# A five-part rewrite of the first stage of a graph network kernel: where the small factor's products, the zeros and the angles are computed

## The reference, cut to what matters

```python
h = jnp.maximum(_layernorm(x, axis=-1), 0.0)
x = x + L0(h)      # h @ W_conv (512x128), summed over edges with dinv*w*dinv, + b_conv, @ W_lin + b_lin
# for layer 2, depends on the noise levels alone:
ph = noise_levels * freqs                       # 625 x 32
emb = concatenate([sin(ph), cos(ph)])           # 625 x 64
cond = silu(emb @ f_w1 + f_b1) @ f_w2 + f_b2    # 625 x 16
```

## Time and profile before

| what | value |
|---|---|
| three runs | 974.55, 974.86, 977.94 us, median 974.86 |
| profiled execution, its own time | 974.24 us |
| its span | 972.2 us |
| mean granted TensorE clock | 0.967 of full |
| busy share of the span | PE 88%, DVE 69%, POOL 53%, ACT 46% |
| chain that ended last | PE 56%, DVE 20%, POOL 7%, issue 6%, ACT 5% |

### The profile page before, as it was taken

One profiled execution on the slowest core, in us unless ns is written; L12 is line 12 of the kernel. 1 busy time (PEld: TensorE's weight loads), 2 busy tenths in 40 slices (PEclk: granted clock), 3 DMA queues, 4 the chain that ended last, 5 costly groups with the idle time before them and its releaser, 6 DMA issues.

```text
span 972.2 us, 18314 instructions
## 1 busy us (share of the span) xinstructions
PE 860.0 (88%) x6780; PEld 752.3 (77%) x6780; DVE 672.2 (69%) x1311; ACT 451.4 (46%) x760; POOL 519.3 (53%) x598
## 2 busy tenths in 40 slices
PE   0799976998999989999989999989999998889787
PEld 0498875886989877999877898878798988765456
DVE  8689978786267676356577337677526767779986
ACT  1277754323466233456323347522346625245564
POOL 6357744345843176753266663236684319537771
PEclk9999997999999999999999999999999999978998
DMA  4000000204310016220003430001431002100111
GB/s 114 23 23 0 0 22 22 68 16 104 98 34 1 1 34 162 68 65 1 1 22 101 113 104 2 1 22 52 125 102 31 1 1 76 33 1 28 42 56 53
DMA packets 49362, 44.34 MB, mean 46 GB/s; under 512 B 6014, under 2 KB 37154, under 8 KB 49300
## 3 DMA queue, kind: packets, MB, share of 16 engines
q1 hardware_dynamic: 47124, 40.20, 14.2%
q10 hardware_dynamic: 2176, 3.32, 1.8%
HBM read 42.04 MB, written 1.33 MB: 45 GB/s over the span
## 4 chain that ended last, share of the span: by engine, by line
PE 56%; DVE 20%; POOL 7%; issue 6%; ACT 5%; DVEq 2%; SPq 2%; DMA 1%; ACTq 0%; POOLq 0%
PE psum L1583 22%; PE psum L1577 16%; PE psum L1673 8%; PE psum L1601 5%; POOL ringw L1301 3%; DVE arena L2024 2%; ACT arena L1436 2%; DVE arena L902 2%; POOL z L1216 1%; PE psum L824 1%; DVE stats L2168 1%; PE psum L1621 1%; DVEq L2269 1%; DVE hot_dst L939 1%; SPq L1142 1%
## 5 line engine op out<-in xcount | busy, mean ns | idle before, releaser
L1236 POOL TENSOR_SCALAR acc<-acc,rden,flag 128x640 f32<-128x640 f32 x80 | 70.2, 879 | 110.8 <-DVE rden L2020 110.3
L1673 PE MATMUL psum<-ringw,arena 128*128 128x512 f32 x480 | 118.9, 396 | 3.6 <-DVE arena L2032 2.5
L1583 PE MATMUL psum<-ringw,arena 128*128 128x512 f32 (+2 forms) x438 | 105.5, 399 | 12.6 <-POOL ringw L1301 5.2
L1583 PE MATMUL psum<-arena 128*128 128x384 f32 (+3 forms) x675 | 116.0, 325 | 0.4 <-DVE arena L2343 0.4
L1577 PE MATMUL psum<-arena,ringw 128*128 128x320 f32 x768 | 113.3, 309 | 0.0
L1577 PEld LDWEIGHTS psum<-arena,ringw 128*128 128x128 f32 x768 | 113.0, 188 | 0.3
L1583 PEld LDWEIGHTS psum<-arena 128*128 128x128 f32 x675 | 104.7, 189 | 7.7 <-DVE arena L2024 1.1
L1673 PEld LDWEIGHTS psum<-ringw,arena 128*128 128x128 f32 x480 | 87.8, 188 | 23.8 <-DVE arena L2032 3.5
L1583 PEld LDWEIGHTS psum<-ringw,arena 128*128 128x128 f32 x438 | 81.9, 217 | 30.3 <-issue 14.8
L1601 PE MATMUL psum<-ident,acc 128*128 128x128 f32 x560 | 82.1, 278 | 18.8 <-DVE acc L1933 14.7
L1577 PE MATMUL psum<-arena 128*128 128x320 f32 x480 | 88.5, 322 | 6.2 <-DVE arena L2024 5.5
(11 more groups left out here) (280 smaller groups left out, 1836.9 us busy)
## 6 DMA issues: line engine op xcount, KB each, us to landing
...
```

The costliest lines, as they stand in the source:

```text
L1236: g.tensor_scalar(pbuf[:, k % 4, :], pbuf[:, k % 4, :], rden[:, k:k + 1], flag[:, 1, k % NT:k % NT + 1], ALU.mult, ALU.mult).then_inc(pn_u ...
L1583: ins = pe.matmul(to, l, r, start=(i == 0), stop=(i == len(terms) - 1))
L1673: ins = pe.matmul(brow(ROWBLK[f"{name}{t}"]), l, r, start=(pieces[0] + i == 0), stop=(pieces[-1] == KT - 1 and i == len(terms) - 1))
```

## The change

- Zeros of the accumulators: from PoolE (memset) to ScalarE (copy of a broadcast column, scale 0), before its first weight.
- Noise levels load first on ScalarE's queue, without a wait; the 10 other small loads go to SyncE's queue, behind the biases and ahead of the L1 weights.
- Angles: from VectorE to PoolE, 9 instructions, ahead of `rstd_of`. ScalarE takes the absolute value of the cosine half and folds sign and shift into the sine's scale and bias.
- The fills of `fcol` become four small VectorE instructions on the identity, ahead of the edge lists.
- Norm by tile: VectorE takes statistics, normalises and splits tile by tile; TensorE turns tile t + 2 between the products of tile t (`own_features`), which now are 8 per tile, 256 columns wide (both weight parts side by side, all four terms). They lie in banks 4, 5, 6, and VectorE sums the two halves after the loop with 3 reductions (`hsum`, in SBUF), from which h0 is made; ScalarE no longer waits for VectorE there.
- z1's bias and sigmoid on ScalarE straight from PSUM, the gate product on PoolE, cond's high part on ScalarE and `condT` in one VectorE step in place of four.

```diff
-PRE_BIG = ["src", "w", "base", "dst"] + [f"l0_{t}" for t in range(NT)] + ["z1", "cond", "hall"]
+PRE_BIG = ["src", "w", "base", "dst"] + [f"l0_{t}" for t in range(NT)] + ["cond", "pad", "hall"]
...
+wave = sb("wave", [2 * NF, 2], F32)
+pick = sb("pick", [P, 6], F32)
...
+hsum = hot_dst[:, :, :, :].rearrange("p b j n -> p (b j n)").bitcast(F32)[:, NP:2 * NP].rearrange("p (t n) -> p t n", t=NT)
+cond_high = arena1[:, 0:NP]
...
+first_buf = {BIG0["l0_1"]: 0, BIG0["l0_2"]: 1, BIG0["l0_3"]: 0, BIG0["l0_4"]: 1, BIG0["cond"]: 0}
...
+def buf(u):
+    return first_buf.get(u, u % NBIG)
...
-def own_part(u, t):
...
-    return big[u % NBIG][:, t % 2, t // 2 * P:(t // 2 + 1) * P]
...
+def hall_part(t):
...
+    return psum[:, (4, 5, 4, 5, 6)[t], t // 2 % 2 * 2 * P:(t // 2 % 2 + 1) * 2 * P].rearrange("p (s n) -> p s n", s=2)
...
+z1 = psum[0:C16, 2 * NBIG:2 * NBIG + NROW, 0:HALF]
...
+    sp.wait_ge(const1, 4)
+    sp.wait_ge(cb_one, 2)
+    sp.dma_start(f_w1[:, :], a["L2_gnn_f_w1"]).then_inc(f_ld, 16)
+    sp.dma_start(fcol[0:C16, 3:4], a["L2_gnn_f_b1"].unsqueeze(1)).then_inc(f_ld, 16)
+    for i in range(4):
+        sp.dma_start(f_w2[:, 32 * i:32 * i + C16], a["L2_gnn_f_w2"]).then_inc(f_ld, 16)
+        sp.dma_start(fcol[32 * i:32 * i + C16, 2:3], a["L2_gnn_f_b2"].unsqueeze(1)).then_inc(f_ld, 16)
...
-    g.memset(acc[:, 0:NT * ACCW], 0.0).then_inc(scat_read, HOT)
-    g.memset(acc[:, NT * ACCW:2 * NT * ACCW], 0.0).then_inc(scat_full, HOT)
...
-    g.wait_ge(f_ld, 16 * F_LOADS)
-    for i in range(8):
-        if i:
-            g.wait_ge(cb_one, i)
-        g.affine_select(out=fcol[:, 2:3], in_=fcol[:, 2:3], compare_op=ALU.not_equal, fill=1.0,
-                        base=-(32 * (i // 2) + C16 + i % 2), pattern=[[0, 1]], channel_multiplier=1).then_inc(cb_one, 1)
+    for lo, sign, shift in ((0, 1.0, 0.0), (NF, -1.0, float(np.pi / 2))):
+        step(g.memset(wave[lo:lo + NF, 0:1], sign))
+        step(g.memset(wave[lo:lo + NF, 1:2], shift))
...
+    noise, ph, kf, r, part = tmp64
+    step(g.tensor_scalar(fcol[0:2 * NF, 1:2], freq_i, float(np.float32(2.0 * np.pi / 16)), 1.0, ALU.mult, ALU.mult))
+    g.wait_ge(noise_ld, 16)
+    step(g.tensor_scalar(ph, noise, fcol[0:2 * NF, 1:2], 1.0, ALU.mult, ALU.mult))
+    MAGIC = 1.5 * 2.0 ** 23
+    step(g.tensor_scalar(kf, ph, float(1 / (2 * np.pi)), MAGIC, ALU.mult, ALU.add))
+    step(g.tensor_scalar(kf, kf, -MAGIC, 1.0, ALU.add, ALU.mult))
+    TURN_HI = 6.28125
+    step(g.tensor_scalar(part, kf, -TURN_HI, 1.0, ALU.mult, ALU.mult))
+    step(g.tensor_tensor(r, part, ph, ALU.add))
+    step(g.tensor_scalar(part, kf, -float(2 * np.pi - TURN_HI), 1.0, ALU.mult, ALU.mult))
+    step(g.tensor_tensor(r, r, part, ALU.add))
+    g.tensor_scalar(r, r, 3.1415925, -3.1415925, ALU.min, ALU.max).then_inc(emb_up, 1)
...
-    for m in range(2):
-        rest(m, ringpart(m))
+        if t in (1, 2):
+            rest(t - 1, ringpart(t - 1))
+    g.wait_ge(sig_done, 1)
+    g.tensor_tensor(mask[0:C16, 3, :], mask[0:C16, 1, :], mask[0:C16, 2, :], ALU.mult).then_inc(silu_up, 1)
...
+    act.dma_start(tmp64[0][:, 0:N], a["node_vec1"].rearrange("n o -> o n").broadcast_to([2 * NF, N])).then_inc(noise_ld, 16)
+    act.wait_ge(const0, 2)
+    for i, ready in enumerate((scat_read, scat_full)):
+        act.activation(acc[:, i * NT * ACCW:(i + 1) * NT * ACCW], ones[:, 0:1].broadcast_to([P, NT * ACCW]), ACT.Copy,
+                       scale=0.0).then_inc(ready, HOT)
...
-    act.activation(tmp64[4], tmp64[3], ACT.Sin).then_inc(sin_done, 1)
+    act.activation(tmp64[3][NF:2 * NF], tmp64[3][NF:2 * NF], ACT.Abs).then_inc(sin_done, 1)
+    act.wait_ge(sin_done, 1)
+    act.activation(tmp64[4], tmp64[3], ACT.Sin, bias=wave[:, 1:2], scale=wave[:, 0:1]).then_inc(sin_done, 1)
...
+        if t == 1:
+            act.wait_ge(z1_full, 1)
+            act.wait_ge(f_ld, 16 * F_LOADS)
+            act.activation(wide(mask[0:C16, 1, :]), z1, ACT.Identity, bias=fcol[0:C16, 3:4])
+        if t == 2:
+            act.activation(wide(mask[0:C16, 2, :]), z1, ACT.Sigmoid, bias=fcol[0:C16, 3:4]).then_inc(sig_done, 1)
+    u = BIG0["cond"]
+    act.wait_ge(cb_one, 3)
+    act.wait_ge(big_full, u + 1)
+    act.activation(wide(cond_high), bwide(u), ACT.Identity, bias=pick[:, 5:6], scale=pick[:, 4:5]).then_inc(cond_hi, 1)
...
-    act.wait_ge(condT_up, 2)
...
-        if t >= 2:
-            act.wait_ge(h0lo_up, t - 1)
-        act.activation(h0[:, 0, t, :], own_part(BIG0["hall"], t), ACT.Copy, scale=degs[:, 3, t:t + 1]).then_inc(h0hi_up, 1)
+        act.activation(h0[:, 0, t, :], hsum[:, t, :], ACT.Copy, scale=degs[:, 3, t:t + 1]).then_inc(h0hi_up, 1)
...
+    u = ROW0["vec"]
+    pe.wait_ge(vec_ld, 16 * 9)
+    pe.transpose(brow(u)[:, 0:VECS], vec[:, :], ident[0:VECS, 0:VECS]).then_inc(row_full, 1)
...
-    for t in range(NT):
-        turn_norm(BIG0[f"l0_{t}"], t, t)
-    u = ROW0["vec"]
-    pe.wait_ge(vec_ld, 16 * 9)
-    pe.transpose(brow(u)[:, 0:VECS], vec[:, :], ident[0:VECS, 0:VECS]).then_inc(row_full, 1)
...
-    u = BIG0["z1"]
-    free_big(pe, u)
-    pe.wait_ge(sin_done, 1)
+    def turn_first(t):
+        pe.wait_ge(big_read, BIG0[("w", "dst", "l0_0", "l0_1", "l0_2")[t]] + 1)
+        pe.wait_ge(xn_up, t + 1)
+        turn(pe, BIG0[f"l0_{t}"], xn[:, t % 2, :], KT).then_inc(big_full, 1)
...
+    def own_features(t):
+        pe.wait_ge(big_read, BIG0[f"l0_{t}"] + 1)
+        if t == 0:
+            pe.wait_ge(split_done, Q_CONV + 1)
+        weight = ringw[:, Q_CONV, :, :].rearrange("p s (k n) -> p s k n", k=KT)
+        return row_mm(pe, hall_part(t), [(yT[:, s, k, t * P:(t + 1) * P], weight[:, :, k, :]) for k in range(KT) for s in range(2)])
...
+    turn_first(0)
+    turn_first(1)
+    pe.wait_ge(row_read, ROW0["vec"] + 1)
+    pe.wait_ge(sin_done, 2)
...
+        ins = pe.matmul(z1[:, h, :], f_w1[:, :], tmp64[4][:, h * HALF:(h + 1) * HALF], start=True, stop=True)
+    ins.then_inc(z1_full, 1)
+    own_features(0)
+    turn_first(2)
+    own_features(1)
+    turn_first(3)
+    own_features(2)
+    pe.wait_ge(sig_done, 1)
...
-    row_mm(pe, brow(u)[:, :], parts([bc_hl[:, 0, :], bc_hl[:, 1, :]], ringpart(Q_LIN))).then_inc(row_full, 1)
+    row_mm(pe, brow(ROW0["brow"])[:, :], parts([bc_hl[:, 0, :], bc_hl[:, 1, :]], ringpart(Q_LIN))).then_inc(row_full, 1)
+    turn_first(4)
+    own_features(3)
...
-    free_big(pe, u)
+    pe.wait_ge(big_read, BIG0["l0_3"] + 1)
...
-    wide_mm(pe, u, [(f_w2[:, :], mask[0:C16, 3, :])]).then_inc(big_full, 1)
...
-    u = BIG0["hall"]
-    free_big(pe, u)
-    pe.wait_ge(split_done, Q_CONV + 1)
-    pe.wait_ge(big_read, BIG0[f"l0_{NT - 1}"] + 1)
-    for t in range(NT):
-        ins = row_mm(pe, own_part(u, t), sum([parts(tile_of(yT, k, t), wcol(Q_CONV, k)) for k in range(KT)], []))
-    ins.then_inc(big_full, 1)
+    wide_mm(pe, u, [(f_w2[:, :], mask[0:C16, 3, :])]).then_inc(big_full, 2)
+    own_features(4).then_inc(big_full, 1)
...
+    dve.wait_ge(const0, 3)
+    dve.wait_ge(const1, 1)
+    blocks = ident[:, :].rearrange("p (i n) -> p i n", i=4)
+    dve.tensor_reduce(pick[:, 0:4], blocks[:, :, C16:C16 + 2], AX.X, ALU.add).then_inc(cb_one, 1)
+    dve.wait_ge(cb_one, 1)
+    dve.tensor_reduce(fcol[:, 2:3], pick[:, 0:4], AX.X, ALU.add).then_inc(cb_one, 1)
+    dve.wait_ge(cb_one, 2)
+    step(dve.tensor_reduce(pick[:, 0:4], blocks, AX.X, ALU.add))
+    step(dve.tensor_tensor(pick[:, 4:5], pick[:, 1:2], pick[:, 3:4], ALU.add))
...
+    def first_norm(t):
+        if t >= 2:
+            dve.wait_ge(big_full, BIG0[f"l0_{t - 2}"] + 1)
+        normalise(t, t, x[:, t, :], xn[:, t % 2, :])
...
+    def first_stats(t):
+        tile_stats(t, t, x[:, t, :])
...
+    def first_rest(t):
+        turned_rest(BIG0[f"l0_{t}"], t, t)
...
-    for t in range(NT):
-        tile_stats(t, t, x[:, t, :])
...
-    dve.wait_ge(const1, 3)
-    dve.wait_ge(f_ld, 16 * F_LOADS)
-    step(dve.tensor_scalar(fcol[0:2 * NF, 1:2], freq_i, float(np.float32(2.0 * np.pi / 16)), None, ALU.mult))
-    noise, ph, kf, r = tmp64[0:4]
-    step(dve.tensor_scalar(ph, noise, fcol[0:2 * NF, 1:2], None, ALU.mult))
-    MAGIC = 1.5 * 2.0 ** 23
-    step(dve.tensor_scalar(kf, ph, float(1 / (2 * np.pi)), MAGIC, ALU.mult, ALU.add))
-    step(dve.tensor_scalar(kf, kf, MAGIC, None, ALU.subtract))
-    TURN_HI = 6.28125
-    step(dve.scalar_tensor_tensor(r, kf, -TURN_HI, ph, ALU.mult, ALU.add))
-    step(dve.scalar_tensor_tensor(r, kf, -float(2 * np.pi - TURN_HI), r, ALU.mult, ALU.add))
-    step(dve.tensor_scalar(r, r, 3.1415925, -3.1415925, ALU.min, ALU.max))
-    c = r[NF:2 * NF]
-    step(dve.scalar_tensor_tensor(c, c, -1.0, c, ALU.mult, ALU.max))
-    dve.tensor_scalar(c, c, -1.0, float(np.pi / 2), ALU.mult, ALU.add).then_inc(emb_up, 1)
-    relu_norm(0, 0, [BIG0[f"l0_{t}"] for t in range(NT)], 0)
+    first_stats(0)
+    first_stats(1)
+    first_norm(0)
...
+    first_stats(2)
+    first_norm(1)
...
+    first_stats(3)
+    first_rest(0)
+    first_norm(2)
+    first_stats(4)
+    first_rest(1)
+    first_norm(3)
```

(41 more changed lines are left out.)

61 lines of the change are left out of this document (16 added, 45 removed).

## The result

The kernel after takes **962.27 us** (median of four runs, 962.08 to 962.62), the kernel before 975.48 in the same comparison (four runs, 974.55 to 977.94): ratio 0.9861, 95% interval 0.9842 to 0.988, a gain of 13.2 us. The forecast was 966.6 within 960.5 to 971.0, on the likeliest case a gain of 7.65; the gain is about that of the first rival (TensorE's clock rises inside the stage, 963.2 us) and one microsecond more: the result lies in the range, and what the forecast called likeliest did not come. The profiled execution took 962.15 us, its span is 960.3.

A forecast was written before the change was run, and what follows sets the result against it. The chain of waits to VectorE's first one-hot, then VectorE in the loop, was taken as the bound. Entry -8.5, stall -1.25 and h0 parts +2.1 gave -7.65 us on 974.24: 966.6 us, range 960.5 to 971.0.

The forecast's parts named there:

- the first rival: Stage before the loop: TensorE at 2.4 GHz from about 30 us, 3.4 us less, total 963.2 us; chance 0.25.
- Zeros and edge lists, angles: Kernel's start: zeros free 4.4 us, used up covering angles on PoolE; statistics at 16.1, VectorE's 7.2 us angle time saved.
- the third rival: Packed schedule before the loop: more waiting than counted, 3 to 7 us of gain lost, 970 to 974 us; chance 0.15.
- The fear about PoolE's rate: Rival, angle steps on PoolE: one step at the power's rate would be 217 us, total some 1180 us; chance 0.05.
- TensorE's list: TensorE from z1 to cond: all products at 1.2 GHz, tile products 1.75 us a tile, cond ending at 38.7 us.
- The wait for brow: TensorE after brow and a turn: 0.4 us waiting for VectorE, which adds brow to the bias first.
- From cond to the loop: VectorE's entry into the loop: first one-hot at 42.5 in place of 51.0 us, 8.5 us earlier.
- The stall: VectorE's first add in the loop: its 1.25 us wait for TensorE goes.
- After the loop: Reductions cost nothing; h0 low parts alternate with PoolE, so the aggregate's low part comes 2.1 us later relative to the loop.
- The rival without any wait: After the loop: h0's low parts do not wait for PoolE, total 964.5 us; chance 0.12.
- The sum: Whole kernel: -8.5 - 1.25 + 2.1 = -7.65 us on a profiled 974.24 us, giving 966.6 us; chance 0.43.

The follow-up runs named there:

- the narrow run: The kernel after with each 256-column tile product issued as two of 128 columns, same sums and place: 972.73 us, ratio 0.9937 to the kernel before.
- where the loop was entered late: The kernel after with 32 extra one-hot steps of 640 columns on VectorE ahead of the loop: 976.53 us, ratio 0.9989 to the kernel before.

## Why the prediction was right, and where it was off

**Zeros and edge lists, angles: right.** Cast at 5.70 with 0.64 us (forecast: done by 5.7; it started later, as the edge lists landed at 5.6 behind the noise load, which I had only as a mishap of the third rival), statistics at 15.34 (16.1), z1 at 20.84 (21.6). PoolE's multiply steps took 0.72 to 0.79 us and its additions 1.53, against 0.88 and 1.56. The alternation is in the trace: three small VectorE steps of 0.15 to 0.23 us when alone (the run with the angles back) take 0.74, 0.79 and 1.58 beside PoolE. The fear about PoolE's rate for add with a large constant and for min with max had no ground: 0.72 and 0.77 us, and 0.71, for 640 columns. (The power is some 250 times L1236's rate a column and not 380; the 217 us of that rival are right.)

**TensorE's list: the step that failed.** "All products here are at the lower clock, 1.2 GHz" held until just before 27 us and not behind it. Cond ended near 33.7 where the step had 38.7. Of the 5.0 us, 0.8 came from z1's earlier start; the other 4.2 are the clock, in turns at 0.60, products at 1.22 a tile, cond at 1.34, less a longer wait for brow. The rival had priced this at 3.4 us and its mark (turns at 0.6 from about 30 us) came at 27.27. The row that I drew on,'s `hall` at an even 0.217, was one of narrow products, and the narrow run shows that with those it would have held: I had taken the level of one shape for that of another. The wait for brow that I put at 0.4 us was 1.01.

**From cond to the loop: right in mechanism, too low in one term.** ScalarE 0.88, VectorE 0.88; the diagonal copies took 1.7 us where I had 0.65 and 0.4 for PoolE. From cond's end to the first one-hot it was 4.8 us where I had 3.8. First one-hot 12.6 us earlier, not 8.5; the difference of 4.1 is the 5.0 at cond less the 0.9 lost here.

**The stall: right.** 1.25 forecast; 0.94 in the profiled execution (the loop took 85.66 us in place of 86.60), 1.15 where the loop was entered late. TensorE's low clock may be the rest. In ten traces of the kernel after and its edits the loop took 85.66 to 85.69 us where the clock stayed low for 8.4 us or more behind the first one-hot, and 85.45 to 85.56 where it rose sooner or was never low; no run sets the clock apart from the rest. (The eleventh, with the copies and tile 3's low part early, spent 1.0 us more on its first one-hots.)

**After the loop: right in mechanism, mis-sized.** The reductions lie inside VectorE's idle time, 0.45 of the 2.04 us being left. The h0 parts alternate with PoolE's four, forecast to end 6.6 us behind the degrees, measured 5.8 (5.05 us of them); the count parts then take 3.02. Loss 0.8 to 0.9 us in place of 2.1: the lead was 13.5 us at the loop's end, 13.58 at the degrees and 12.67 at the low part of the aggregate. The rival without any wait falls.

**The sum.** By the measured terms -12.57 - 0.94 + 0.84 = -12.67 at the aggregate's low part, against -7.65. The medians differ by 13.2, the profiled spans by 11.9. Behind 160 us the change touches nothing, and yet the lead goes from 12.7 to 15.6 (at the first attention step), to 11.3 at the last. It can be seen at one block's boundary. The kernel before, then the kernel after, TensorE behind the same wait for PoolE:
```profile
687.65 3.00 PE L1583 MATMUL psum<-ringw,arena 128*128 128x512 f32 x12 [1.29 <-POOL ringw L1301]
```
```profile
675.22 4.57 PE L1617 MATMUL psum<-ringw,arena 128*128 128x512 f32 x12 [1.29 <-POOL ringw L1329]
```
The same twelve products behind the same gap take 3.00 us in one and 4.57 in the other, and the windows behind the gap show the granted clock at 1.00 (687 to 692 us) and at 0.66 (675 to 680). Which boundary falls into a lower clock differs from kernel to kernel, and the totals can scatter by it: with the noise load behind the edge lists the first one-hot (38.47) and the loop's end (124.16) stand where they do in the kernel after, and the span is 1.6 us shorter (958.7 against 960.3). What decides where the clock is low was not tried.
